# Widening packed mask pieces on VectorE instead of loading them in a four-layer graph network

## The reference

```python
def reference(x, adj, ...):
    # layer 0: out[b,n] = sum over k of (A_k x)[b,n] @ w_n,k + b_n, with A_0 = 1, A_1 = adj, A_2 = 2 adj adj - 1
    x = _layernorm(x + _L0_gnn_ref(x, adj, L0_gnn_embedding, L0_gnn_weight, L0_gnn_bias))
    # layer 1, twice: z = relu((adj @ z) @ weights[i])
    x = _layernorm(x + _L1_gnn_ref(x, 0, L1_gnn_net_params, adj))
    # layer 2: x @ weight_self + (adj @ x) @ weight_neighbor + bias
    x = _layernorm(x + _L2_gnn_ref(x, adj, L2_gnn_weight_self, L2_gnn_weight_neighbor, L2_gnn_bias))
    # layer 3: x, adj x, 2 adj adj x - x, concatenated, @ weight + bias (both supports are adj)
    x = _layernorm(x + _L3_gnn_ref(x, adj, adj, L3_gnn_weight, L3_gnn_bias))
    return x
```

## Time and profile before

| | |
|---|---|
| median of three runs | 1213.95 us (1209.44 to 1216.85) |
| the profiled execution | 1218.93 us |
| its span in the trace | 1217.1 us |
| busy share of the span: PE, PEld, DVE, ACT, POOL | 96%, 80%, 67%, 42%, 28% |
| loads of ready pieces (`B<-tf`) | 77 of 512 KB |
| stores of ready pieces (`tf<-B`) | 15 of 512 KB |
| widenings on ACT, on DVE | 266, 25 |

### The profile page before, as it was taken

One profiled execution on the slowest core, in us unless ns is written; L12 is line 12 of the kernel. 1 busy time (PEld: TensorE's weight loads), 2 busy tenths in 40 slices (PEclk: granted clock), 3 DMA queues, 4 the chain that ended last, 5 costly groups with the idle time before them and its releaser, 6 DMA issues.

```text
span 1217.1 us, 16608 instructions
## 1 busy us (share of the span) xinstructions
PE 1173.1 (96%) x5539; PEld 969.2 (80%) x5539; DVE 813.3 (67%) x1773; ACT 509.2 (42%) x687; POOL 336.5 (28%) x208
## 2 busy tenths in 40 slices
PE   9999999999999999899999999999999999988996
PEld 6888888888888887777888787888888887866875
DVE  5935897877768877998347357788657574733544
ACT  6622111120111101110156666677666766743665
POOL 0001111010105553654121113244536241410312
PEclk9999999999999999999999999999999999989998
DMA  9832112241214221221543454525654166687563
GB/s 364 328 104 62 40 45 73 64 102 34 62 60 113 70 70 44 82 66 52 172 180 139 158 174 149 170 98 158 150 139 121 34 152 163 162 221 215 170 218 107
DMA packets 181453, 154.77 MB, mean 127 GB/s; under 512 B 121520, under 2 KB 141520, under 8 KB 180080
## 3 DMA queue, kind: packets, MB, share of 16 engines
q1 hardware_dynamic: 170272, 113.24, 31.3%
q10 hardware_dynamic: 11088, 40.38, 10.4%
HBM read 109.01 MB, written 44.56 MB: 126 GB/s over the span
## 4 chain that ended last, share of the span: by engine, by line
PE 78%; DVE 8%; DMA 5%; SPq 5%; issue 2%; ACT 1%; POOL 0%; POOLq 0%; DVEq 0%; ACTq 0%
PE ps L1630 20%; PE ps L1207 15%; PE ps L1209 15%; PE ps L1517 8%; PE ps L1518 8%; PE ps L1535 7%; SPq L1447 4%; DMA B<-tf 3%; PE ps L1565 2%; PE ps L1566 2%; DVE nat L1937 2%; DVE ring L1937 2%; DMA ring_g<-td 1%; DVE xs L1916 1%; SPq L1495 1%
## 5 line engine op out<-in xcount | busy, mean ns | idle before, releaser
L1207 PE MATMUL ps<-B,ops 128*128 128x512 f32 x1008 | 403.8, 401 | 13.8 <-DMA B<-tf 11.8
L1209 PE MATMUL ps<-B,ops 128*128 128x512 f32 x1008 | 395.3, 392 | 0.0
L1259 ACT CAST B<-pk 128x1024 fp32r<-128x1024 fp8e4 (+1 forms) x266 | 262.1, 1020 | 139.7 <-PE ps L1209 136.0
L1630 PE MATMUL ps<-Tw,xs 128*128 128x512 f32 x1280 | 309.6, 391 | 7.6 <-DVE ring L1937 7.3
L1630 PEld LDWEIGHTS ps<-Tw,xs 128*128 128x128 f32 x1280 | 238.2, 188 | 64.7 <-DVE ring L1937 9.6
L1207 PEld LDWEIGHTS ps<-B,ops 128*128 128x128 f32 x1008 | 191.0, 189 | 59.6 <-DMA B<-tf 17.9
L1209 PEld LDWEIGHTS ps<-B,ops 128*128 128x128 f32 x1008 | 191.0, 189 | 36.8
L1517 PE MATMUL ps<-B,xs 128*128 128x512 f32 x512 | 200.3, 391 | 0.7 <-DVE xs L1838 0.7
L1518 PE MATMUL ps<-B,xs 128*128 128x512 f32 x512 | 199.3, 389 | 0.0
L1937 DVE SCALAR_TENSOR_TENSOR nat<-ps,embn,nat 128x128 f32<-128x128 f32 x448 | 152.8, 341 | 40.6 <-PE ps L1630 39.9
L1937 DVE SCALAR_TENSOR_TENSOR ring<-ps,embn,ring 128x128 f32<-128x128 f32 x512 | 174.3, 340 | 0.0
(11 more groups left out here) (121 smaller groups left out, 1191.7 us busy)
## 6 DMA issues: line engine op xcount, KB each, us to landing
B<-tf ACTq DMA_DIRECT2D x77, 512.0 KB, 3.6
raw<-in_at SPq DMA_DIRECT2D x10, 1024.0 KB, 15.2
td<-raw SPq DMA_DIRECT2D x33, 256.0 KB, 2.6
tf<-B SPq DMA_DIRECT2D x15, 512.0 KB, 2.6
raw<-in_at SPq DMA_DIRECT2D x12, 512.0 KB, 8.7
zd<-nat SPq DMA_DIRECT2D x24, 256.0 KB, 3.0
stg<-zd SPq DMA_DIRECT2D x24, 256.0 KB, 5.2
tb<-stq SPq DMA_DIRECT2D x40, 128.0 KB, 2.2
```

Of the source, the lines that this page charges most:

```text
L1207: pe.matmul(bank, ops[:, slot, 0, m, :], of, start=not more and m == 0, stop=False, skip_group_check=more)
L1209: mm = pe.matmul(bank, ops[:, slot, 1, m, :], of, start=False, stop=m == 7, skip_group_check=more)
L1259: eng.copy(to, of).then_inc(s_exA, 1)
L1630: mm = pe.matmul(ps[:, 4 + 2 * p + q, :], src, Tw[:, wi, 512 * p:512 * p + 512], start=i == 0, stop=i == 4)
```

## The change

Layer 6 no longer loads any piece; ScalarE and VectorE widen all of them, VectorE three of eight. Layers 3 and 4 load only pieces 0, 1, 2 and 16, 17, 18 of the 40; the pieces that were loaded elsewhere go to VectorE (11 in a pass of layer 3, 5 in a pass of layer 4). The strings are now 40 letters long. Only six pieces are stored in P0 instead of 15. The last weighing of the last pass stands at slot 28 instead of 29, which moves the steps that follow from it (`plus`, `square`, `deviation`, `root`, `unit`, `ship`) one slot forward too. The very last scaling runs on VectorE instead of GpSimd, with its own semaphore for SP.

```diff
--- before.py
+++ after.py
@@ -446,9 +446,10 @@
 KEPT = {0: 2, 1: 1, 2: 0}
 
 
-EXPANDS = {2: "AAVAAVAV", 3: "AADAADAD", 4: "AADAAAAD", 5: "AAAAAAAV", 6: "AADAADAD"}
-
-STASHED = [k for k in range(40) if EXPANDS[6][k % 8] == "D"]
+
+EXPANDS = {2: "AAVAAVAV" * 5, 3: "DDDAAVAAVAAVAAVADDDAAVAAVAAVAAVAAVAAVAAV", 4: "DDDAAAAAAVAAAAAVDDDAAAAAAVAAAAAVAAAAAVAA", 5: "AAAAAAAV" * 5, 6: "AAVAAVAVAAVAAVAVAAVAAVAVAAVAAVAVAAVAAVAV"}
+
+STASHED = [k for k in range(40) if "D" in (EXPANDS[3][k], EXPANDS[4][k], EXPANDS[6][k])]
 
 RING = [8, 9, 10, 11, 15]
 
@@ -487,12 +488,12 @@
 
 AHEAD = {4: 7, 5: 5}
 
-LAST_WEIGH = [17, 18, 21, 22, 25, 26, 27, 29]
+LAST_WEIGH = [17, 18, 21, 22, 25, 26, 27, 28]
 
 
 def expander(e):
 
-    return EXPANDS[PASSES[e // 40][1]][e % 8] if e < 40 * len(PASSES) - 8 else "A"
+    return EXPANDS[PASSES[e // 40][1]][e % 40] if e < 40 * len(PASSES) - 8 else "A"
 
 
 def chunks(n):
@@ -1014,6 +1015,7 @@
                 mean2_at = numbered(FAST, "mean", start=len(mean_at))
                 square_at = numbered(FAST, "square", start=len(mean_at))
                 dev_at, unit2_at = (numbered(FAST, kind, start=first_var) for kind in ("deviation", "unit"))
+                last_unit = max(unit2_at, key=unit2_at.get)
                 turn2_at = numbered(FAST, "flip", "yflip", start=len(turn_at))
                 biased_at = numbered(FAST, "biased")
                 dense_at = {s.c: i + 1 for i, s in enumerate(complete) if (s.j, s.p) == (3, 2)}
@@ -1378,6 +1380,9 @@
                         sm, g = stats(j, c), home(j, c).rearrange("p (g k) -> p g k", k=C)
                         dv.wait_ge(s_std, dev_at[s._replace(kind="deviation")])
                         dv.reciprocal(sm[:, 0, :], sm[:, 3, :]).then_inc(s_rec, 1)
+                        if s == last_unit:
+                            dv.wait_ge(s_rec, unit2_at[s])
+                            dv.tensor_tensor(g, g, sm[:, 0, :].unsqueeze(2).to_broadcast([P, 8, C]), ALU.mult).then_inc(s_a2, 1)
 
                 def pool_step(po, s):
 
@@ -1428,7 +1433,7 @@
                                              ALU.subtract).then_inc(s_raw, 1)
                         if x == S3:
                             po.tensor_tensor(to, home_half(2 * g, 0), home_half(2 * g + 1, 0), ALU.subtract).then_inc(s_raw, 1)
-                    if s.kind == "unit":
+                    if s.kind == "unit" and s != last_unit:
                         sm, g = stats(j, c), home(j, c).rearrange("p (g k) -> p g k", k=C)
                         po.wait_ge(s_rec, unit2_at[s])
                         po.tensor_tensor(g, g, sm[:, 0, :].unsqueeze(2).to_broadcast([P, 8, C]), ALU.mult).then_inc(s_norm, 1)
@@ -1498,7 +1503,10 @@
                         sp.wait_ge(*stored_at["yflip", j, p, c])
                         blocks_back(sp, home(j, c), td[j, 1, c], s_h[j][c])
                     if s.kind == "ship":
-                        sp.wait_ge(s_norm, unit2_at[s._replace(kind="unit")])
+                        if s._replace(kind="unit") == last_unit:
+                            sp.wait_ge(s_a2, len(plus_at) + 1)
+                        else:
+                            sp.wait_ge(s_norm, unit2_at[s._replace(kind="unit")])
                         sp.dma_start(out[j, :, cols], home(j, c)).then_inc(s_h[j][c], 16)
 
                 def sp_end(sp):
```

## The result

The changed kernel takes 1200.52 us (median of four runs, 1199.36 to 1201.57); the kernel before, run beside it, 1214.53 us. The ratio is 0.988, with a 95% interval of 0.986 to 0.990. The forecast was 1198, with 1187 to 1209 around it. Further down, two executions (1673 and 1676 us at a granted clock of 0.66, one of the kernel with layer six's old loads, one of that with 512 KB transfers beside P7) are left out of the medians.

What follows compares the result with a forecast made beforehand. TensorE was taken as the bound, losing 34.5 us in six passes to waits for loads and late flipped blocks and to clock falls. Terms summed to 18.5 us, corrected to 16: 1198 us against the 1213.95 median, range 1187 to 1209.

Steps and rivals of the forecast that it cites:

- P0: First of the second half's nine passes: casts no longer wait for a store; gain 0.7 of 1.8 us, bounds 0 and 1.2.
- P7: Eighth of the nine passes: no waits for loads, flipped blocks land sooner; 5.5 us loss left, gain 10.8, bounds 15.3 and 4.
- The fourth weighing: Last of four weighings that P7 inherits from layer five; forecast 2.8 us late, the others on time or 0.3 late.
- Now cast 10 stands ahead of that flip: VectorE's queue in P7: the cast waits for a product ending two units later, delaying the flip 2.5 us more.
- Refills beside the landing: Layer six's refills run beside the landing of the fourth weighing's block in P7; part of its 2.8 us lateness.
- SP bounds P7: Rival: SP's ordered issues keep weighings late, P7 gains 4, 1204 us; chance 0.26, shared with casts eating part of the gain.
- P8: Last of the nine passes: twelve casts instead of loads, loss 1.3 us; gain 2.4, bounds 3.2 and 0.
- P1, P2: Second and third passes: last cast 1 to 1.5 us late, loss 2.0 each; gains 2.1 and 2.8, bounds 3.6, 4.3 and 0.
- P3: Fourth pass, with P4 the fifth: ten costless loads become six loads and five casts; 0.4 us lost each, bounds 0 and 2.
- The end: After the last product: earlier last weighing and sum, last scaling on VectorE; gain 0.5 us, bounds 0 and 0.9.
- VectorE as the bound: Rival: casts in P1, P2, P7 and P8 meet GpSimd's work, come 2 to 3 us late; 1232 us, chance 0.08.
- The correction: Whole sum: profiled execution was 5.0 us above the median; half of that comes off the 18.5 us gain, leaving 16.

## Why the prediction was right, and where it was not

**P7, 10.8 forecast, 10.8 measured.** The exact size is partly luck. The direction holds: transfers beside P7 make its flipped blocks late, and the kernel with unread transfers shows that this is enough for a loss of this size. The prediction had split the loss into 4.4 us of waits for loads and the rest; in that kernel the products wait for nothing and the weighings 14.0 us, where before they waited 5.9 (5.1 of it in the earlier trace rows). So the two parts are not independent terms. The landing itself came back as forecast for the block of the weighing that was 4.2 us late before: its last load took 5.91 us then and 2.54 in the changed kernel, and that weighing is on time. Of the loss that should be left, 0.5 + 2.8 + 1.0 + 1.2 = 5.5, the trace has 5.4, but made up otherwise: nothing for the other weighings, 3.7 for the fourth, some 1.7 for the clock's single fall (half of 3.41 us), and nothing for the fifteen casts, which stand unchanged in the kernel with the later refills, whose P7 has no wait at all.

The fourth weighing's reason was wrong. "Now cast 10 stands ahead of that flip" changes nothing as long as SyncE is not there sooner. What the chain of the prediction left out: it counted VectorE's 1.35 us and SyncE's 6.0 as if SyncE were free when the flip is, though the earlier trace rows has SyncE's stretch as a term of its own. In the changed kernel the chain from the end of the weighing two before (1073.20) is 4.1 us to the flip's store, 5.8 to the first issue, 2.1 to the last and 4.5 of landing; the prediction had 1.35 + 2.5, 6.0, 2.6 and 2.6. The first term was near, but it was SyncE's earlier steps and not the cast; the mis-sized one is the landing. "Refills beside the landing", put at 0.3 us, cost 1.8 us of landing and 2.0 ahead of the issue.

So the rival "SP bounds P7" was right about the place and wrong about the size: SyncE is the engine without free time in the first half of P7, but it gets through its order sooner when nothing runs beside it (5.8 us for the five steps, 12.5 beside the unread transfers). (In the kernel before, the same steps for the fourth weighing took 6.0 us and the weighing was 1.1 late: there TensorE had lost its time earlier in the pass, to another weighing, 4.2 us, and to loads.)

**P8 and P1, P2: better than forecast.** 3.7 for 2.4, and 3.0 and 3.7 for 2.1 and 2.8. The prediction charged 0.1 us for each cast spread over the pass. In P8 no product waited, with twelve casts, and in P1 and P2 the idle times sum to 0.7 us each, of which piece 39 is 0.5, where 1.2 was forecast for it. So most casts cost nothing, and 0.1 for each was an average over a few that come late. P1's 3.0 is in part the fall of the clock in one execution: with the old loads it came to 60.1, so 0.8 is what the two kernels show.

**P3: the failed term.** "Ten loads that cost nothing become six loads and five casts: 0.4 each, bounds 0 and 2." P4 lost 0.6 (0.1 by the kernel with the old strings), P3 2.0, at the upper bound. It was sized by an average over casts instead of by the queue, which had been followed for P1 and P2 only. Followed here, it has the split of X12 ahead of piece 15's cast, and that split waits for ScalarE.

**P0**: 0.8 for 0.7, by the mechanism named: no cast waits for a store (`tf<-B`) any more, and with the old strings P0 is back at 57.2.

**The end**: -0.6 for +0.5. The step that failed is "its sum stands ahead of the deviation of the chunk before instead of behind it": I took that as a gain for the last chunk and did not ask what it does to the chunk before. That chunk's store moves back by 0.55 us, close ahead of the last one, whose issue then takes 0.63 us longer, more than the 0.40 us by which it starts earlier. The scaling on VectorE did finish earlier; beside GpSimd's scaling it took 1.17 us and not 0.69, as the prediction had feared.

**VectorE as the bound** did not come about. Of 84 casts, 65 had no instruction of GpSimd beside them and took 685 ns in the mean, at most 695. The other 19 took 1163 ns in the mean and 2031 at most:

```profile
L1265 DVE CAST B<-pk x84: 634/686/2031, 625.0 to 1171.9; 128x1024 fp32r<-128x1024 fp8e4 x84
...
  PEld ps L1209: 9.2, 11
  PE ps L1209: 5.1, 8
```

The rule weighed in the prediction (Trainium skill, SBUF — State Buffer, section "Who interferes with whom") asks for this, and the trace agrees, but most of the long casts lay where TensorE had its piece in time. The 9.2 us that weight loads waited are just above the 4 to 9 that the prediction named; only 5.1 reached the matmuls, and the largest of it was piece 15 of P3, not piece 39. The forecast that `ring_g<-td` lands in 2.5 to 3.5 us in P7 missed as well: it was 2.5 to 5.0.

**The correction.** The terms summed to 18.5; the passes show 19.1. Taking half of the 5.0 us off the gain, because the profiled execution was above the median, gave 16; the timed gain is 14.0. The profiled execution of before was slower than its median by more than 4 us, that of after by 1.

## What to carry to other kernels

A load that arrives just in time may cost little by itself and much by what it does to the other transfers of the pass: add unread transfers of the same size to see that price alone. Look for the engine without a gap, here SyncE with a queue in fixed order; moving four of its transfers behind the urgent ones gave 5.4 us in a pass (4.6 with piece 14 moved as well), where a step ahead of it done 3 us sooner gave nothing. And an instruction in a fixed order is priced by the one it is queued behind, not by its own mean.

## What was not expected of the hardware

SyncE's issues are not of fixed length. The four issues of 64 KB ahead of P7's fourth weighing took 2.63 us without transfers of ScalarE beside them, 3.83 us with 256 KB ones, and 5.74 us with 512 KB (not every group is held up: the next two of four in that kernel took 2.60 and 2.63):

```profile
1078.43 3.83 SPq L1460 DMA_DIRECT2D stg<-td  x4
```

That row is of the kernel with the smaller transfers. Transfers issued by one engine thus take issue time from another. The same shows at the span's end with SyncE's own: the last store's issue took 0.33 us when the store before it was 1.48 us ahead, 0.59 at 1.00 us, and 0.66 to 1.08 at 0.55 (all thirteen kernels).
